# Bilinear corners summed by accumulating transposes on TensorE, and keys/values projected from 64-row tiles

## The reference, cut to what matters

```
# x0i, y0i: upper left corner of a sampling point, wx, wy: its fraction
v00 = gather(y0i, x0i);      v01 = gather(y0i, x0i + 1)
v10 = gather(y0i + 1, x0i);  v11 = gather(y0i + 1, x0i + 1)
sampled = v00*(1-wx)*(1-wy) + v01*wx*(1-wy) + v10*(1-wx)*wy + v11*wx*wy   # [B, 1024, 8, 64]
keys    = einsum('bnpc,dc->bnpd', sampled, W_k)      # and values with W_v
scores  = einsum('bnhd,bnphd->bnhp', q, k) / sqrt(8)
out     = einsum('bnhp,bnphd->bnhd', softmax(scores), v)
```

## Time and profile of the kernel before

| | |
|---|---|
| median of the runs | 3222.56 us |
| span of the profiled execution | 3792.6 us |
| TensorE (PE), busy | 2490.2 us |
| VectorE (DVE), busy | 2526.8 us |
| ScalarE (ACT), busy | 1933.1 us |
| GpSimd (POOL), busy | 2306.9 us |

### The profile page before, as it was taken

How to read it: one execution, slowest core, us unless ns; L and a number is a source line. 1 busy time by engine, 2 the same in 40 slices (tenths; PEclk the granted TensorE clock), 3 DMA queues, 4 the chain that set the end, 5 groups by cost and what they waited for, 6 DMA issues and landing times.

```text
span 3792.6 us, 38290 instructions
## 1 busy us (share of the span) xinstructions
PE 2490.2 (66%) x10390; PEld 1540.7 (41%) x10424; DVE 2526.8 (67%) x3121; ACT 1933.1 (51%) x4630; POOL 2306.9 (61%) x2052
## 2 busy tenths in 40 slices
PE   3456667576676756667575766757666675766678
PEld 2334344343443434344343444434343443434433
DVE  3757678575676857668585767857576685766661
ACT  2445455464554546445454645646454454645564
POOL 4565766657576665767656576665757566575700
PEclk7778878797897978789787877978788787887889
DMA  4232322323232232322323233232323223232300
GB/s 128 78 94 75 96 87 68 102 72 105 78 96 77 77 104 71 105 86 84 92 71 99 75 100 91 68 99 71 103 78 105 73 78 102 69 96 71 87 8 11
DMA packets 139221, 315.82 MB, mean 83 GB/s; under 512 B 68896, under 2 KB 69152, under 8 KB 134816
## 3 DMA queue, kind: packets, MB, share of 16 engines
q0 software_dynamic: 98304, 268.57, 24.4%
q1 hardware_dynamic: 40736, 45.58, 3.7%
HBM read 305.62 MB, written 8.40 MB: 83 GB/s over the span
## 4 chain that ended last, share of the span: by engine, by line
DVE 22%; another core or an unknown queue 21%; issue 20%; PE 17%; ACT 12%; POOL 7%; DMA 1%; DVEq 0%; ACTq 0%; SPq 0%; POOLq 0%
POOL gathered L451 7%; PE work_ps L466 5%; DVE gathered L1034 5%; ACT gathered L707 4%; PE points_ps L515 3%; PE work_ps L574 2%; DVE products L1063 2%; DVE gathered L1037 2%; DVE products L1047 2%; DVE scores L1050 1%; PE work_ps L604 1%; PE kv_ps L526 1%; ACT wide L780 1%; ACT sampled_t L715 1%
## 5 line engine op out<-in xcount | busy, mean ns | idle before, releaser
L451 POOL DMA_INDIRECT gathered<-pixels,index x2048 | 2306.7, 1126 | 1302.1 <-issue 604.7
L707 ACT ACTIVATE gathered<-gathered,mix 128x64 f32<-128x64 f32 x2048 | 513.9, 340 | 278.1 <-DMA gathered<-pixels,index 251.3
L515 PE MATMUL points_ps<-c_sb,gathered 128*128 128x128 f32 x2048 | 373.0, 332 | 394.4 <-DVE gathered L1037 264.9
L715 ACT ACTIVATE sampled_t<-points_ps 128x512 f32<-128x512 f32 x512 | 285.9, 599 | 632.1 <-remote 386.7
L526 PE MATMUL kv_ps<-w_sb,sampled_t 128*128 128x128 f32 x4096 | 516.5, 284 | 103.7 <-issue 63.3
L1047 DVE TENSOR_TENSOR products<-kv_ps,queries 128x1024 f32<-128x1024 f32 x128 | 156.3, 1221 | 633.2 <-remote 625.5
L526 PEld LDWEIGHTS kv_ps<-w_sb,sampled_t 128*128 128x128 f32 x4096 | 502.7, 200 | 137.3 <-issue 89.5
L515 PEld LDWEIGHTS points_ps<-c_sb,gathered 128*128 128x128 f32 x2048 | 303.0, 172 | 532.2 <-issue 393.4
L466 PE MATMUL work_ps<-hn,w_sb 128*128 128x512 f32 x544 | 378.2, 819 | 201.5 <-ACT xc L770 93.3
L1034 DVE TENSOR_TENSOR gathered<-gathered,mix 128x1536 f32<-128x1536 f32 x256 | 449.2, 1755 | 38.7 <-issue 30.4
L1037 DVE TENSOR_TENSOR gathered<-gathered 128x1024 f32<-128x1024 f32 x256 | 313.7, 1225 | 28.1 <-issue 0.4
(11 more groups left out here) (168 smaller groups left out, 3345.9 us busy)
## 6 DMA issues: line engine op xcount, KB each, us to landing
grid_px<-grid SPq DMA_DIRECT2D x32, 1024.0 KB
gathered<-pixels,index POOLq DMA_INDIRECT x2048
out<-rm SPq DMA_DIRECT2D x32, 256.0 KB
w_sb<-weights SPq DMA_DIRECT2D x1, 2176.0 KB, 7.7
moe_hidden<-consts SPq DMA_DIRECT2D x1, 512.0 KB, 8.3
attended<-cls SPq DMA_DIRECT2D x1, 512.0 KB, 11.9
c_sb<-consts SPq DMA_DIRECT2D x1, 192.0 KB, 8.4
s_sb<-shape_vectors SPq DMA_DIRECT2D x1, 96.0 KB, 8.4
```

Source lines behind the costliest of these rows:

```text
L451: pool.indirect_dma_start(gathered[:, n % RING, k * PATCH:(k + 1) * PATCH], None, pixels, bass.IndirectOffsetOnAxis(ap=index[:, n // TILES ...
L515: mm = pe.transpose(points_ps[:, h, k * P:(k + 1) * P], g[:, 4 * h + k, 0:2 * C], ident)
L707: ins = act.activation(g[:, at, :], g[:, at, :], ACT.Copy, scale=wt)
L715: act.activation(sampled_t[:, n % 2, 4 * h:4 * h + 4, :].rearrange("p k n -> p (k n)"), points_ps[:, h, :], ACT.Copy).then_inc(points_copi ...
```

## The change

- `weighed`, a buffer of its own with two halves, takes the weighted corners; they are no longer written in place. In it each pair of points (2j, 2j+1) has, for each corner q, a block of 128 columns: the 64 channels of the one point and the 64 of the other.
- VectorE multiplies 24 of the 32 blocks as before, now in two instructions: all 4 corners of the even points (16 blocks) and the first 2 of the odd ones (8 blocks). ScalarE multiplies the last 2 corners of the odd points (8 blocks).
- The addition of the lower to the upper row on VectorE is gone, and with it VectorE's wait for its own product and for ScalarE.
- TensorE makes 16 transpositions a tile, not 8: the four corners of a pair of points are accumulated in the same columns of PSUM. A tile's 8 points then fill one bank, not two.
- ScalarE copies one bank a tile, not two.
- Each point now lies in 64 rows. `project` makes one product for each point, with 64 rows of `sampled_t` and of `W_KV`; even points use rows 0 to 63, odd ones rows 64 to 127, in turn.
- A ring slot is free for GpSimd once both VectorE and ScalarE have weighed its tile.
- `scores` also serves for `shifted` and `attended_raw`, which are gone.

```diff
-SCALAR_CORNERS = 8
+VECTOR_CORNERS = 2
-        sampled_t = sb("sampled_t", [P, 2, HEADS, P])
+        weighed = sb("weighed", [P, 2, HEADS * PATCH])
+        sampled_t = sb("sampled_t", [P, 2, HEADS // 2, P])
...
-                    pool.wait_ge(points_full.sem, points_full.at(it, 2 * (n - RING) + 2))
+                    pool.wait_ge(weighted.sem, weighted.at(it, n - RING + 1))
+                    pool.wait_ge(corners_weighed.sem, corners_weighed.at(it, n - RING + 1))
...
             def sample(it, n):
                 pe.wait_ge(weighted.sem, weighted.at(it, n + 1))
-                g = gathered[:, n % RING, :].rearrange("p (k n) -> p k n", k=HEADS)
-                for h in range(2):
-                    pe.wait_ge(points_copied.sem, points_copied.at(it, 2 * n + h - 1))
-                    for k in range(4):
-                        mm = pe.transpose(points_ps[:, h, k * P:(k + 1) * P], g[:, 4 * h + k, 0:2 * C], ident)
-                    mm.then_inc(points_full.sem, 1)
+                pe.wait_ge(corners_weighed.sem, corners_weighed.at(it, n + 1))
+                pe.wait_ge(points_copied.sem, points_copied.at(it, n - 1))
+                for j in range(HEADS // 2):
+                    for q in range(4):
+                        at = (4 * j + q) * 2 * C
+                        mm = pe.matmul(points_ps[:, n % 2, j * P:(j + 1) * P],
+                                       weighed[:, n % 2, at:at + 2 * C], ident, is_transpose=True,
+                                       start=(q == 0), stop=(q == 3))
+                mm.then_inc(points_full.sem, 1)
...
-                    for h in range(2):
-                        pe.wait_ge(points_copied.sem, points_copied.at(it, 2 * n + h + 1))
-                        for k in range(4):
-                            mm = pe.matmul(kv_ps[:, 2 * (n % 2) + h, k * P:(k + 1) * P],
-                                           sampled_t[:, n % 2, 4 * h + k, :], w(W_KV), start=True, stop=True)
-                        mm.then_inc(kv_full.sem, 1)
+                    pe.wait_ge(points_copied.sem, points_copied.at(it, n + 1))
+                    for j in range(HEADS // 2):
+                        for e in range(2):
+                            rows = slice(e * C, (e + 1) * C)
+                            mm = pe.matmul(kv_ps[:, 2 * (n % 2) + e, j * P:(j + 1) * P],
+                                           sampled_t[rows, n % 2, j, :], w_sb[rows, W_KV, :], start=True, stop=True)
+                            if j == HEADS // 2 - 1:
+                                mm.then_inc(kv_full.sem, 1)
...
             # ScalarE, weigh_corners and copy_points
+                act.wait_ge(points_full.sem, points_full.at(it, n - 1))
+                g, to = corners_of(s), weighed_of(n)
+                for j in range(HEADS // 2):
+                    for q in range(VECTOR_CORNERS, 4):
+                        wt = mix[:, b, t, 2 * j + 1, q:q + 1]
+                        ins = act.activation(to[:, j, q, 1, :], g[:, j, 1, q, :], ACT.Copy, scale=wt)
...
+                act.activation(sampled_t[:, n % 2, :, :].rearrange("p j n -> p (j n)"),
+                               points_ps[:, n % 2, :], ACT.Copy).then_inc(points_copied.sem, 1)
...
             # VectorE, weigh
-                step(dve.tensor_tensor(g[:, 0:own, :], g[:, 0:own, :], wt, ALU.mult))
-                dve.wait_ge(corners_weighed.sem, corners_weighed.at(it, n + 1))
-                g = gathered[:, s, :].rearrange("p (k n) -> p k n", k=HEADS)
-                dve.tensor_tensor(g[:, :, 0:2 * C], g[:, :, 0:2 * C], g[:, :, 2 * C:4 * C], ALU.add).then_inc(weighted.sem, 1)
+                dve.wait_ge(points_full.sem, points_full.at(it, n - 1))
+                g, to = corners_of(s), weighed_of(n)
+                wt = mix[:, b, t, :, :].rearrange("p (j e) q -> p j e q", e=2)
+                for e, own in ((0, 4), (1, VECTOR_CORNERS)):
+                    ins = dve.tensor_tensor(to[:, :, 0:own, e, :], g[:, :, e, 0:own, :],
+                                            wt[:, :, e, 0:own].unsqueeze(3).broadcast_to([P, HEADS // 2, own, C]),
+                                            ALU.mult)
+                ins.then_inc(weighted.sem, 1)
```

More of the change, by code:

```diff
@@ L161, in vit_kernel @@
     first_looped, last_looped = 2, pairs - 2
-    VECTOR_STEPS, SCALAR_STEPS = 113, 18
+    VECTOR_STEPS, SCALAR_STEPS = 97, 18
     all_parts = (1, 2, "q0", "q1")
@@ L219, in vit_kernel @@
         gathered = sb("gathered", [P, RING, HEADS * PATCH])
-        sampled_t = sb("sampled_t", [P, 2, HEADS, P])
+        weighed = sb("weighed", [P, 2, HEADS * PATCH])
+        sampled_t = sb("sampled_t", [P, 2, HEADS // 2, P])
         products = sb("products", [P, 2, HEADS, C])
         scores = sb("scores", [P, 2, HEADS, HEADS])
-        shifted = sb("shifted", [P, 2, HEADS, HEADS])
         top = sb("top", [P, 2, HEADS])
@@ L226, in vit_kernel @@
         prob_sum = sb("prob_sum", [P, 2, HEADS])
-        attended_raw = sb("attended_raw", [P, 2, C])
         attended = sb("attended", [P, TILES, 2, C])
@@ L286, in vit_kernel @@
         weighted = signal("weighted", PAIR_TILES)
-        points_full = signal("points_full", 2 * PAIR_TILES)
-        points_copied = signal("points_copied", 2 * PAIR_TILES)
+        points_full = signal("points_full", PAIR_TILES)
+        points_copied = signal("points_copied", PAIR_TILES)
         kv_full = signal("kv_full", 2 * PAIR_TILES)
@@ L338, in cols, with corners_of, weighed_of @@
             return slice(h * HALF, (h + 1) * HALF)
+        def corners_of(s):
+            return gathered[:, s, :].rearrange("p (j e q c) -> p j e q c", e=2, q=4, c=C)
+        def weighed_of(n):
+            return weighed[:, n % 2, :].rearrange("p (j q e c) -> p j q e c", q=4, e=2, c=C)
         def fill(eng, it, part, name, *inputs):
@@ L703, in weigh_corners @@
                 act.wait_ge(slot_gathered[s].sem, slot_gathered[s].at(it, (n // RING + 1) * HEADS * 16))
[L704 to L707, removed]
+                act.wait_ge(points_full.sem, points_full.at(it, n - 1))
[4 more added lines that the diff above has]
+                        ins = act.activation(to[:, j, q, 1, :], g[:, j, 1, q, :], ACT.Copy, scale=wt)
                 ins.then_inc(corners_weighed.sem, 1)
             def copy_points(it, n):
-                for h in range(2):
-                    act.wait_ge(points_full.sem, points_full.at(it, 2 * n + h + 1))
-                    act.wait_ge(kv_full.sem, kv_full.at(it, 2 * (n - 2) + h + 1))
-                    act.activation(sampled_t[:, n % 2, 4 * h:4 * h + 4, :].rearrange("p k n -> p (k n)"),
-                                   points_ps[:, h, :], ACT.Copy).then_inc(points_copied.sem, 1)
+                act.wait_ge(points_full.sem, points_full.at(it, n + 1))
+                act.wait_ge(kv_full.sem, kv_full.at(it, 2 * (n - 2) + 2))
+                act.activation(sampled_t[:, n % 2, :, :].rearrange("p j n -> p (j n)"),
+                               points_ps[:, n % 2, :], ACT.Copy).then_inc(points_copied.sem, 1)
             def exponentials(it, m):
                 act.wait_ge(scores_ready.sem, scores_ready.at(it, m + 1))
-                act.activation(probs[:, :, :, :], shifted[:, :, :, :], ACT.Exp,
+                act.activation(probs[:, :, :, :], scores[:, :, :, :], ACT.Exp,
                                scale=DH ** -0.5).then_inc(probs_ready.sem, 1)
@@ L1054, in score @@
                                        AX_X, ALU.max))
-                dve.tensor_tensor(shifted[:, :, :, :], scores[:, :, :, :],
+                dve.tensor_tensor(scores[:, :, :, :], scores[:, :, :, :],
                                   top[:, :, :].unsqueeze(2).broadcast_to(shape),
@@ L1069, in attend @@
                 dve.wait_ge(values_used.sem, values_used.at(it, m + 1))
-                mark(dve.tensor_reduce(attended_raw[:, :, :], products[:, :, :, :].rearrange("p t k c -> p t c k"),
+                mark(dve.tensor_reduce(scores[:, :, :, :].rearrange("p t k h -> p t (k h)"), products[:, :, :, :].rearrange("p t k c -> p t c k"),
                                        AX_X, ALU.add))
@@ L1077, in attend @@
                 dve.tensor_tensor(attended[:, t:t + 2, b, :].rearrange("p t (h d) -> p t h d", h=HEADS),
-                                  attended_raw[:, :, :].rearrange("p t (h d) -> p t h d", h=HEADS),
+                                  scores[:, :, :, :].rearrange("p t k h -> p t (k h)").rearrange("p t (h d) -> p t h d", h=HEADS),
                                   prob_sum[:, :, :].unsqueeze(3).broadcast_to([P, 2, HEADS, DH]),
```

3 lines of the change are left out of this document (removed).

## The result

The changed kernel takes 3083.52 us (median of 4 runs, 3079.33 to 3090.7) against 3223.0 us (4 runs) of the kernel before: ratio 0.9568, 95% interval 0.9552 to 0.9584. That is 139 us less; the forecast was 3070 us, 152 us less.

A forecast was written before the change was run, and what follows sets the result against it. It took no engine alone as the bound: VectorE, TensorE and GpSimd near 150 to 160 of 189 us an iteration. VectorE -19, TensorE +23 - 8 gave 179 us an iteration, 152 us won in all: 3070 us, range 2930 to 3235.

The forecast's parts named there:

- The 570 us between span and median: Profiled execution 3792.6 us against median 3222.56 us; taken mostly for pauses from recording, so 189 us an iteration, not 225.
- The bound: In the sampling loop, VectorE, TensorE and GpSimd stand near 150 to 160 of 189 us an iteration; none bounds alone.
- VectorE's work: Weighing a tile falls from 3.10 to 1.91 us: 19 us less an iteration, 305 us in all.
- GpSimd beside VectorE: Gathers stretched beside two-input SBUF steps win 0.3 us in 8 tiles an iteration, 38 us in all; bounds 0 and 0.6.
- Transpositions: TensorE's 8 more a tile cost 1.04 to 1.97 us; mean taken, 23 us an iteration, 373 us in all.
- 64-row products: TensorE's projections with 64 rows for 128: a quarter off, 8 us less an iteration, 130 us in all.
- The drain on a change of mode: At TensorE's projections, worst case: nothing overlaps and switching adds 0.5 us a burst, 4 us an iteration.
- TensorE's busy time: In the whole trace, up by 150 to 350 us; per iteration from 148 to 163 us.
- Rival D: Slower: TensorE is the bound already and VectorE's saving goes to nobody; 3358 us, or 3489 without projection gain; chance 0.18.
- C: TensorE takes up all but a rest of the gain: 3190 us, from 3150 to 3230; chance 0.17.
- Slots freed earlier: GpSimd refills a slot once weighed: part of its 290.1 us wait goes, but by itself little, as indices come next.
- Rival B: TensorE has room, so all of VectorE's 305 us are won: 2918 us, with GpSimd's share 2900; chance 0.15.

The follow-up runs named there:

- e5: The kernel before, unchanged, profiled again on a chip where it takes its median time: 3229.23 us.
- e2: The kernel before without VectorE's addition, TensorE itself waiting for ScalarE's weighing: 3202.64 us, ratio 0.9942 to the kernel before.
- e8: The changed kernel with VectorE's 24 blocks multiplied in one instruction of 1536 elements: 3201.39 us, ratio 0.9925 to the kernel before.
- e3: The changed kernel with each projection multiplying all 128 rows, same count of matmuls: 3079.98 us, ratio 0.956 to the kernel before.
- e4: The changed kernel with 8 more transpositions a tile, 24 in all: 3083.71 us, ratio 0.9559 to the kernel before.
- e7: The kernel before with VectorE's multiplication in two and its addition left out: 3079.62 us, ratio 0.9554 to the kernel before.
- e11: The changed kernel with the 512-element multiplication before the 1024-element one, on a chip where the kernel before takes 3783.81 us: 4039.71 us, ratio 1.0677.
- e6: The kernel before with VectorE's multiplication in two, of 1024 and 512 elements, the addition kept: 3229.54 us, ratio 1.0018 to the kernel before.
- e10: The changed kernel plus a 1024-element reduction (one SBUF input) after each tile's multiplications, on a chip where the kernel before takes 3783.81 us: 4089.69 us, ratio 1.0815.

## Why the prediction was right in the number and wrong in the reason

The forecast was 152 us less, the measured difference is 139. Point by point:

- **The 570 us between span and median.** Taken for the cost of recording. Wrong: e5 is recorded and takes 3229 us. In all runs on record they go with the chip, two of four. Everything read from the earlier trace rows about who waits was read from an execution that the median does not contain.
- **The bound.** "None is the bound alone", with GpSimd at 145 of 189 us. Wrong, and the step that failed is a sum. GpSimd was counted short twice: at 160 us an iteration, 128 undisturbed gathers with their pauses but without what holds them up, and in the sum at 142 us, the busy time without the 0.30 us pause after each gather. With both, it has 145 + 38 = 183 of 189 us, 97%, and stands far ahead of VectorE's 155. The rows had it.
- **VectorE's work.** 3.10 to 1.91 us a tile: 1222 + 682 ns measured, busy time 2526.8 to 2234.0 us where about 2225 was forecast. Right in size, and nobody waited for it: e2 takes 304 us away for 20, e8 puts the long instruction back for 118.
- **GpSimd beside VectorE.** Here is the whole gain, sized at 0.3 us a tile in half of the tiles, 38 us. Measured 0.62 us a tile ((324 - 165) / 256) in all of them, the upper bound of 0.6, because GpSimd never waits. The mechanism was named and mis-sized by a factor of four. It was also put down to the addition that goes, which by itself is worth 33 us of held gathers (324 to 291, e2); the cut of the multiplication, without which 118 of the 139 us are gone (e8), was given nothing. And the one tile of the earlier trace rows, with 0.6 us lost, was a mild one: the mean of e5 is 324 / 256 = 1.27 us. The 0.82 us could be read there already: the gather of 1245.62 ends at 1246.99, the multiplication beside it at 1246.17. The 152 us came from VectorE's saving, halved by TensorE, which is not what happens. The halving hit the number by chance. The page of the Trainium skill that I set beside it (SBUF — State Buffer, the shared port pair) also says that the loser blocks until the other's instruction is over. The rows above agree, with the 0.82 us after each end; had I followed it, the length of the single instruction, not its existence, would have been in the sum.
- **Transpositions.** 2.29 us for 16 (587.5 / 256), against 1.27 for 8 in e5: 262 us more in all, forecast 373. An accumulating one costs no more than another.
- **64-row products.** A quarter off was taken, 43% came off against e5 (491.8 to 278.0 us), near the best case, 2.2 us for a burst of 32. A single one takes no less (288 ns on the mean, 280 in e3), but 4096 fill 278.0 us in place of 494.8, so they run beside each other. That agrees with the concurrent row groups of the Trainium skill (TensorE: Matmul & The Clock Gate, Packing small matmuls). The drain on a change of mode that the prediction took from the Trainium skill (TensorEngine Tiling (Array Packing), Key Properties) is small beside it, if it is there; no run here shows it by itself. Worth nothing in this kernel (e3).
- **TensorE's busy time** was to rise by 150 to 350 us. It fell, 2348.2 to 2330.3 us, and has room for 2048 matmuls more (e4). Rival D (TensorE the bound) falls with that, and so does C. The mean granted clock went up, 0.874 to 0.900, and to 0.925 with 2048 transpositions more (e4). The rule of the Trainium skill (TensorE: Matmul & The Clock Gate, PE-mode transpose) that a transposition does not count as activity would have brought it down; the measurement decides against it here.
- **Slots freed earlier.** "By itself it gives little": e5 never waits for a slot, and e7 has the gain without it.
- **Rival B**, all of VectorE's 305 us won, had the condition that TensorE has room. It has; but the bound was elsewhere.

## What to carry to other kernels

When the span of a profile and the measured times differ by more than a few per cent, the trace may be of an execution of another kind: before reading its waits, add up for each engine what no wait can take away, with the fixed pauses between its instructions, and see which sum comes near the measured time. Where GpSimd's gathers are the bound, a VectorE instruction with two inputs in SBUF is paid by the length that a gather meets; one edit of the pattern can be worth nothing and two together everything, so try them together. Count the step behind them, too: in e11 it took back what the new order gave. Time a change on more than one chip if an engine that it loads more is one that pauses on some.

## What the runs showed of the hardware

- A gather of 128 rows by indices (128 x 1 KB) takes 0.945 us with 0.30 us after it when nothing disturbs. Started inside a VectorE step with two SBUF inputs, it ends 0.81 to 0.83 us after that step's end, in before, e6, after and e11 alike (0.75 us after the scans of L1095, L1105 and L1108 in e5, 49 gathers). Started beside a step with one SBUF input it is not held: 0.945 us on the mean beside the reductions of e10, 0.946 beside a multiplication that reads PSUM (e5).
- Matmuls with 64 rows, in turn on the lower and the upper half, fp32: 278.0 us for 4096 (after), against 494.8 with 128 rows on the same operands (e3).
- Transpositions that accumulate in PSUM, fp32: 306 ns each on the mean (after), those that overwrite 311 ns (e5).
- The same program takes 3216 to 3230 us on two chips and 3772 to 3800 us on two others. On the latter TensorE pauses again and again between matmuls that wait for nothing, in e11's rows for 1.7 to 2.5 us.
